# A decoder layer with attention, a state-space scan and a feed-forward net: scan, gate and feed-forward in halves of 256 tokens

## The chip, the core and the metric

The program runs on one core of a Trainium2 chip. Its engines work side by side and meet at semaphores: TensorE (PE in the profile; PEld is its weight load) multiplies matrices into PSUM, VectorE (DVE) does elementwise work, reductions and scans, ScalarE (ACT) activations, GpSimd (POOL) here only tiny powers and the DMAs that add, SyncE (SP) issues loads and stores. The metric is the device time of one execution in microseconds (us). Three runs of the kernel before took 1647.77, 1651.23 and 1653.64 us, median 1651.23.

## The reference

Four batches of 512 tokens with 512 features, all float32. First attention (16 query heads, 2 key heads, rotary positions, causal softmax) is added to x. Then a state-space block reads a context, is gated by the normed x, and is added. Last comes a feed-forward net with two of eight low-rank experts a token. The core of the scan, for each of 512 channels and 16 states n:

```python
def step(state, inp):
    d, b, c, u = inp
    dA = jnp.exp(d[..., None] * A)
    state = state * dA + (d * u)[..., None] * b[:, None, :]
    y = jnp.einsum('bdn,bn->bd', state, c)
    return (state, y)
_, ys = jax.lax.scan(step, state0, (dt_t, B_t, C_t, u_t))
```

The output y (channels by tokens) is multiplied by silu of the normed x, read as 512 rows by 512 columns: a row of the normed x is a channel of y, a column a token. The feed-forward net computes silu(x Wg) * (x Wu) over 1408 inner features, with adapters for both chosen experts, and a down product, also with adapters.

## The kernel before

Tokens stand in four tiles of 128 (NT), channels in four tiles of 128 (JT), the 1408 inner features in eleven tiles of 128 (FT). Each engine has its own program, written out by hand in the order in which it shall run. The order of the scan's work among the rest is set by tables (`plan`, PLAN_FIRST, PLAN_NEXT): each slot of the program gets some **pieces**.

The scan of a batch has 60 pieces on VectorE. Twelve of them, `poly`, evaluate the logarithm in softplus over all 2048 elements a partition and end in dt and dt*u. Then, for each of the 16 states n, follow `mul` (dt*u times B, L1086), `run` (the scan along the tokens, all four channel tiles in one row of 2048, L1091) and `out` (times C, L1096). ScalarE makes the decay factors for each n (L583) and loads the rows of B and C. GpSimd adds each product to y by an accumulating DMA of 1 MB (L487), each waiting for the one before; `mul` of n waits for the add of n - 2, whose buffer it takes.

A batch goes through these stages:

- **attention**: 32 steps (two heads at a time, key width growing from 128 to 512), each with scores (L820, L823), maximum (L1126), exponentials (L625), transposes and value products; then four output projections (L873), the first sum and the norm of x for the gate.
- **start** of the feed-forward: the gated y (L1179, L1183) is turned (L882), added (L1191), normed (L1028), turned again (L765); the router's logits (L924) go to VectorE, which picks two experts by some twenty tiny operations (L1215 to L1241); masks are turned (L934) and multiply the low-rank product (L940).
- **tiles**: for each inner tile f the base passes (L894: gate and up, four products each, 16 passes in the trace, since a float32 product is two passes), the adapters of the first and second expert (L906), the adapters' down part (L914). After each of the three, ScalarE and VectorE evaluate gate times up (L677, L1260, L1267). 33 such evaluations a batch. `base` of f + 2 waits for the last evaluation of f, whose PSUM banks it takes.
- **down**: eleven products (L974), with the next batch's query, key and value projections between them, then the sums that end the batch (L1280), on which the next attention's first scores wait.

The next batch's context part (input projection, convolution, dt) and most of its scan are done beside the feed-forward of the batch before: 30 pieces in the tiles, 22 in the down stage, 8 in attention. Batch 0 has no feed-forward before it: 13 pieces stand beside its projections, 47 in its attention. The last batch's feed-forward has no scan beside it.

## Time and profile before

| | us |
|---|---|
| median of three runs | 1651.23 |
| the profiled execution | 1649.75 |
| its span, first to last instruction | 1647.9 |
| TensorE busy | 1406.0 |
| VectorE busy | 1218.4 |
| ScalarE busy | 604.9 |
| adding DMAs (1 MB), issue to landing, median | 9.7 |

The mean granted TensorE clock was 0.876 of full speed. The span runs from the first to the last instruction of one profiled execution; the run's own time is 1.85 longer. Of a group of instructions the rows give busy time, mean duration, and how long its engine stood idle before them and what ended that.

### The profile page before, as it was taken

Reading aid. Unit: us, or ns where it says so; the run is one execution under the profiler, and the core shown is the slowest. Engines: PE = TensorE matmul, PEld = TensorE weight load, DVE = VectorE, ACT = ScalarE, POOL = GpSimd, SP = SyncE. Lnnn points to the kernel's source line nnn. Section 1 sums busy time; section 2 is a strip of 40 time slices with the busy share of each in tenths; the row PEclk is TensorE's granted clock in tenths of the full one; section 3 lists DMA queues with packets and bytes.
Section 4 is the critical chain, followed back from the end, with each engine's and each line's share of the span. In section 5 each row is a group of like instructions: output and inputs, shape, how many; then the busy total and the mean of one; then the engine's idle time right before and its main releaser. Section 6 shows DMA issues by size and latency. Waiting matters only on the chain.

```text
span 1647.9 us, 16148 instructions
## 1 busy us (share of the span) xinstructions
PE 1406.0 (85%) x5768; PEld 685.0 (42%) x5768; DVE 1218.4 (74%) x1411; ACT 604.9 (37%) x1436; POOL 111.9 (7%) x116
## 2 busy tenths in 40 slices
PE   5756767999888799899889699899879788799999
PEld 2333433443333354444334255444334345454434
DVE  4899996589989766759998865759998967623330
ACT  5165553323223584232232376242333267211110
POOL 0000001001100000000110000100210000100000
PEclk8855558999999699899999779899999869789999
DMA  4167761123666631112656822012556741101112
GB/s 185 39 147 153 154 141 27 44 66 108 143 141 166 166 66 26 39 50 78 159 128 159 196 68 52 26 37 84 124 131 152 173 135 27 26 13 64 48 32 83
DMA packets 53278, 158.81 MB, mean 96 GB/s; under 512 B 5072, under 2 KB 10704, under 8 KB 44752
## 3 DMA queue, kind: packets, MB, share of 16 engines
q0 software_dynamic: 9216, 67.11, 19.8%
q1 hardware_dynamic: 25664, 54.23, 9.9%
q10 hardware_dynamic: 18320, 36.45, 8.6%
q8 instruction: 47, 0.77, 0.2%
q14 instruction: 31, 0.25, 0.0%
HBM read 86.20 MB, written 4.46 MB: 55 GB/s over the span
## 4 chain that ended last, share of the span: by engine, by line
DVE 30%; issue 30%; PE 29%; DMA 6%; ACT 4%; POOL 2%; DVEq 0%; ACTq 0%; POOLq 0%
DVE state L1091 11%; DMA y_sb<-state 5%; PE ps_a L894 5%; DVE state L1086 4%; PE ps_a L974 4%; PE ps_a L820 3%; DVE state L1096 3%; PE ps_b L834 3%; PE ps_w L873 3%; PE ps_a L906 3%; POOL rstd L477 2%; PE ps_b L914 2%; PE ps_w L782 2%; ACT r L625 2%; DVE neg_max L1126 2%
## 5 line engine op out<-in xcount | busy, mean ns | idle before, releaser
L894 PE MATMUL ps_a<-xt,w_sb 128*128 128x512 f32 x704 | 319.2, 607 | 0.0
L1091 DVE TENSOR_TENSOR_SCAN state<-decay,state 128x2048 f32<-128x2048 f32 x64 | 282.8, 4418 | 5.3 <-ACT decay L583 0.5
L677 ACT ACTIVATE r<-ps_a 128x512 f32<-128x512 f32 x132 | 78.6, 596 | 380.6 <-PE ps_a L906 202.8
L894 PEld LDWEIGHTS ps_a<-xt,w_sb 128*128 128x128 f32 x704 | 138.1, 197 | 174.9 <-issue 174.9
L820 PE MATMUL ps_a<-r 32*128 32x512 f32 (+3 forms) x512 | 140.4, 634 | 81.7 <-ACT r L625 55.2
L906 PE MATMUL ps_a<-r,wb_sb 128*128 128x512 f32 x352 | 177.1, 628 | 35.9 <-DVE r L1267 33.7
L583 ACT ACTIVATE decay<-dt_sb,decay_rate 128x511 f32<-128x511 f32 x256 | 162.9, 712 | 104.9 <-DVE state L1096 72.2
L1260 DVE SCALAR_TENSOR_TENSOR r<-r,ps_a 128x512 f32<-128x512 f32 x132 | 89.9, 681 | 146.3 <-ACT r L677 146.3
L625 ACT ACTIVATE r<-ps_a,neg_max 128x128 f32<-128x128 f32 (+3 forms) x256 | 133.6, 534 | 116.6 <-DVE neg_max L1126 116.1
L974 PE MATMUL ps_a<-wd_sb,r 128*128 128x512 f32 x352 | 162.4, 613 | 0.0
L1086 DVE TENSOR_TENSOR state<-du_sb,bc_sb 128x2048 f32<-128x2048 f32 x64 | 146.3, 2286 | 4.7 <-DMA y_sb<-state 4.6
L1096 DVE TENSOR_TENSOR state<-state,bc_sb 128x2048 f32<-128x2048 f32 x64 | 145.9, 2280 | 0.7
L834 PE MATMUL ps_b<-cst,r 128*128 128x128 f32 x640 | 121.4, 333 | 26.0 <-ACT xt L637 16.8
L906 PEld LDWEIGHTS ps_a<-r,wb_sb 128*128 128x128 f32 x352 | 67.4, 197 | 131.1 <-issue 124.7
L1126 DVE TENSOR_REDUCE neg_max<-ps_a 128x2 f32<-128x256 f32 (+3 forms) x128 | 104.0, 814 | 21.1 <-PE ps_a L823 20.2
L487 POOL DMA_DIRECT2D y_sb<-state x64 | 56.1, 876 | 752.5 <-DVE state L1096 676.9
L974 PEld LDWEIGHTS ps_a<-wd_sb,r 128*128 128x128 f32 x352 | 70.1, 200 | 88.8 <-issue 86.8
L834 PEld LDWEIGHTS ps_b<-cst,r 128*128 128x128 f32 x640 | 89.9, 174 | 34.7 <-issue 29.5
L914 PE MATMUL ps_b<-r,ad_sb 128*128 128x512 f32 x176 | 89.8, 635 | 13.5 <-DVE r L1267 13.5
L820 PEld LDWEIGHTS ps_a<-r 32*128 32x128 f32 x512 | 49.9, 237 | 118.4 <-ACT r L625 77.2
L1267 DVE TENSOR_TENSOR r<-r,ps_a 128x512 f32<-128x512 f32 x132 | 90.7, 687 | 9.6
L477 POOL TENSOR_TENSOR rstd<-var_eps,cst 128x1 f32<-128x1 f32 x48 | 56.0, 1167 | 576.4 <-DVE var_eps L1024 576.4
(120 smaller groups left out, 1475.7 us busy)
## 6 DMA issues: line engine op xcount, KB each, us to landing
y_sb<-state POOLq DMA_DIRECT2D x64, 1024.0 KB, 9.7
bc_sb<-bc_rows ACTq DMA_DIRECT2D x64, 512.0 KB, 5.1
w_sb<-in_w_tiles SPq DMA_DIRECT2D x44, 512.0 KB, 3.7
wd_sb<-in_w_down SPq DMA_DIRECT2D x44, 256.0 KB, 3.5
wb_sb<-in_w_adapt SPq DMA_DIRECT2D x44, 128.0 KB, 2.1
xa<-in_x SPq DMA_DIRECT2D x4, 1024.0 KB, 5.2
out_x<-xb SPq DMA_DIRECT2D x16, 256.0 KB, 7.0
xn_att<-in_ctx_t SPq DMA_DIRECT2D x4, 512.0 KB, 6.1
```

The lines of the kernel that those rows point to most:

```text
L583: nc.scalar.activation(decay[:, n % 2, j, 1:L], dt_sb[:, j, 1:L], ACT.Exp, scale=decay_rate[:, j, n:n + 1]).then_inc(decay_ready, 1)
L625: nc.scalar.activation(probs[:, (2 * s + k) % 4, 0:(i + 1) * P], score_place(s, k), ACT.Exp, bias=neg_max[:, s % 2, k:k + 1], accum_out=ro ...
L820: nc.tensor.matmul(score_place(s, k), q_t[rows, m, i * P:(i + 1) * P], k_t[rows, 0:width], start=True, stop=False, tile_position=(rows.sta ...
L834: mm = nc.tensor.transpose(ps_b[:, k, kt * P:(kt + 1) * P], probs[:, (2 * s + k) % 4, kt * P:(kt + 1) * P], ident)
L894: mm = nc.tensor.matmul(ps_a[:, 2 * (f % 2) + half, :], w_sb[:, slot, at + k * P:at + (k + 1) * P], xt[:, k, :], start=(k == 0), stop=Fals ...
L906: mm = nc.tensor.matmul(ps_a[:, 2 * (f % 2) + half, :], wb_sb[:, f % 2, at:at + P], low[:, 2 * half + k - 1, :], start=False, stop=(k == 2 ...
L914: mm = nc.tensor.matmul(ps_b[:, k - 1, :], ad_sb[:, f, :], hk[:, (2 * f + k - 1) % 4, :], start=(f == 0), stop=(f == FT - 1), skip_group_c ...
L974: mm = nc.tensor.matmul(ps_a[:, i, :], hb[:, f, i * P:(i + 1) * P], wd_sb[:, f % 2, :], start=(f == 0), stop=False, skip_group_check=True)
L1086: tt(state[:, n % 2, :, :], du_sb[:], row, ALU.mult).then_inc(scan_chain, 1)
L1091: nc.vector.tensor_tensor_scan(flat, decay[:, n % 2, :, :].rearrange("p j l -> p (j l)"), flat, 0.0, ALU.mult, ALU.add).then_inc(scan_chai ...
L1096: tt(state[:, n % 2, :, :], state[:, n % 2, :, :], row, ALU.mult).then_inc(scan_chain, 1)
L1126: nc.vector.tensor_reduce(neg_max[:, s % 2, :], both, AX.X, ALU.max, negate=True)\
```

## The change

Everything behind attention is done in **units** of 256 tokens, two a batch (`HALVES = 2`, `HL = 256`).

- *Scan.* `mul`, `run` and `out` work on 4 x 256 tokens. For the first half, the last state of each channel goes to a small table `carry`; for the second half it is copied into column 0 of the state, where the first half has a zero. Each unit has 48 such pieces; the twelve `poly` pieces stay at full width, once a batch. `out` writes to a buffer of its own (`prod`), which the adding DMA reads, so now `out` of n waits for the add of n - 2. An add carries 512 KB, a load of B and C 256 KB.
- *Where the pieces stand.* First half: 12 `poly` in the evaluations 6 to 17 of the second unit before, 20 in its down stage, 28 in the steps of attention (batch 0: 13 and 47, as before). Second half: 14 in eleven slots z0 to z10 between the end of attention and the first unit's masks, 26 in the evaluations of the batch's own first unit, 8 in its first five down slots.
- *Gate.* One operation gates a half for all rows (`gate_y`), after that half's last add. The second unit's gate stands ahead of the sums that close the first (`finish`).
- *Feed-forward.* Two inner tiles share one step (`pair_tiles`): gate and up of a tile stand side by side in one PSUM bank, so one evaluation covers 2 x 256 columns. There are 18 evaluations a unit, the last pair has one tile. Base, adapter and low-rank products stream 256 columns. Weight tiles are loaded once a unit, so twice a batch, into four buffers instead of two.
- *Next batch.* Its context part stands beside the second unit alone: `project_x` at evaluation 2, dt at 4 and 5, the four attention norms at 9, 11, 13 and 15.

```diff
+HALVES = 2
+HL = L // HALVES
+HT = NT // HALVES
+UNITS = BATCH * HALVES
+FP = (FT + 1) // 2
+WS = 4
...
+STATE_PIECES = [(kind, n) for n in range(NS) for kind in ("mul", "run", "out")]
+Z_COUNTS = [1, 1, 1, 1, 1, 1, 2, 1, 2, 1, 2]
...
+            _where = list(zip([("e", _u - 1, e) for e in range(6, EVALS)], spread_over(NPOLY + 2, EVALS - 6)))
+            _where += list(zip([("d", _u - 1, f) for f in range(FT)], spread_over(20, FT)))
+        _rest = len(_pieces) - sum(count for _, count in _where)
+        _where += list(zip([("s", _b, s) for s in range(STEPS - 1)], spread_over(_rest, STEPS - 1)))
+    else:
+        _where = list(zip([("z", _b, k) for k in range(ZSLOTS)], Z_COUNTS))
+        _where += list(zip([("e", _u - 1, e) for e in range(1, EVALS)], spread_over(26, EVALS - 1)))
+        _rest = len(_pieces) - sum(count for _, count in _where)
+        _where += list(zip([("d", _u - 1, f) for f in range(5)], spread_over(_rest, 5)))
...
+            def base(u, p):
+                if p >= 2:
+                    pe.wait_ge(h_ready, u * EVALS + EVAL_AT[p - 2, 2] + 1)
+                elif u > 0:
+                    pe.wait_ge(x3_ready, HT * u)
+                for w, f in enumerate(pair_tiles(p)):
+                    q = u * FT + f
+                    pe.wait_ge(w_loaded[q % WS], 16 * (q // WS + 1))
+                    for half, at in ((0, WG), (1, WU)):
+                        for k in range(KT):
+                            mm = nc.tensor.matmul(ps_a[:, pair_bank(p) + w, half * HL:(half + 1) * HL],
+                                                  w_sb[:, q % WS, at + k * P:at + (k + 1) * P], xt2[:, k, :],
+                                                  start=(half == 0 and k == 0), stop=False, skip_group_check=True)
...
+                if kind == "mul":
...
+                    if h > 0:
+                        dve.wait_ge(carried, b * NS + n + 1)
+                        nc.vector.tensor_copy(state[:, slot, :, 0:1], carry[:, n, :].unsqueeze(2)).then_inc(edge_ready, 1)
...
+            def gate_y(u):
+                b, h = divmod(u, HALVES)
+                cols = slice(h * HL, (h + 1) * HL)
+                dve.wait_ge(z_chain, b * NT + NT)
+                dve.wait_ge(y_added, 16 * NS * (u + 1))
+                stt(silu_z[:, :, cols], y_sb[:, h, :, :], 0.5, silu_z[:, :, cols], ALU.mult, ALU.mult)\
+                    .then_inc(gated_ready, 1)
...
+                    weigh_down(u)
+                    for f in range(FT):
+                        if c is not None:
+                            rotate(c, f)
+                        pieces(("d", u, f))
+                    if first:
+                        gate_y(u + 1)
+                    finish(u)
```

On TensorE, this is the start of a feed-forward before, from the last output projections to the second base product (L739 is the next batch's input projection, L747 and L756 its x and dt products):

```order
L873 MATMUL ps_w<-wo_sb,r 128x512 x8
L739 MATMUL ps_w<-xn_att,win_sb 128x512 x6
L882 MATMUL ps_w<-cst,r 128x128 x16
L739 MATMUL ps_w<-xn_att,win_sb 128x512 x2
L765 MATMUL ps_w<-cst,r 128x128 x16
L924 MATMUL ps_b<-wr_sb,xt 128x8 x16
L894 MATMUL ps_a<-xt,w_sb 128x512 x8
L934 MATMUL ps_w<-cst,r 128x128 x16
L940 MATMUL ps_w<-xt,lora_sb 128x512 x8
L747 MATMUL ps_b<-state,wx_sb 128x512 x4
L906 MATMUL ps_a<-r,wb_sb 128x512 x2
```

And this is the same place after, for the first unit of a batch (L904 output projection, L915 and L923 the two turnings, L930 router, L944 base, L976 masks, L984 low-rank, L956 adapters):

```order
L904 MATMUL ps_w<-wo_sb,r 128x512 x8
L915 MATMUL ps_w<-cst,silu_z 128x128 x8
L923 MATMUL ps_w<-cst,r 128x128 x8
L930 MATMUL ps_b<-wr_sb,r 128x8 x8
L944 MATMUL ps_a<-r,w_sb 128x256 x16
L976 MATMUL ps_w<-cst,r 128x128 x8
L984 MATMUL ps_w<-r,lora_sb 128x256 x8
L956 MATMUL ps_a<-r,wb_sb 128x256 x4
```

The next batch's products have moved to the second unit; what is left has half the columns, and the whole sequence comes twice a batch.

On VectorE, in the tiles before, one full period of an inner tile, once the scan pieces have begun (L1260 and L1267 are an evaluation):

```order
L1260 SCALAR_TENSOR_TENSOR r<-r,ps_a 128x512
L1267 TENSOR_TENSOR r<-r,ps_a 128x512
L1086 TENSOR_TENSOR state<-du_sb,bc_sb 128x2048
L1091 SCALAR_TENSOR_TENSOR state<-decay,state 128x2048
L1260 SCALAR_TENSOR_TENSOR r<-r,ps_a 128x512
```

And in the first unit's tiles after (L1300 and L1305 an evaluation, L1143 `out`, L1122 the carry's copy, L1125 `mul`, L1132 `run`):

```order
L1300 SCALAR_TENSOR_TENSOR r<-r,ps_a 128x512
L1305 TENSOR_TENSOR r<-r,ps_a 128x512
L1143 TENSOR_TENSOR area<-area,bc_sb 128x1024
L1300 SCALAR_TENSOR_TENSOR r<-r,ps_a 128x512
L1305 TENSOR_TENSOR r<-r,ps_a 128x512
L1122 COPY area<-carry 128x4
L1125 TENSOR_TENSOR area<-du_sb,bc_sb 128x4x256
L1132 SCALAR_TENSOR_TENSOR area<-area 128x1028
```

The whole pieces between two evaluations have become half pieces, in turn one and two behind each evaluation.

Between the end of attention and the router, VectorE now has pieces too. Before, from the last gated tile:

```order
L1179 SCALAR_TENSOR_TENSOR r<-r 128x512
L1183 SCALAR_TENSOR_TENSOR r<-y_sb,r 128x512
L1191 TENSOR_TENSOR xb<-ps_w,xa 128x512
L1018 BN_STATS stats<-xb 128x6
L1021 COPY scrap<-vec 1x1
```

After, from the last row of the gate on (L1197 silu, L1222 the gate, L1230 the second sum):

```order
L1197 SCALAR_TENSOR_TENSOR silu_z<-silu_z,r 128x512
L1143 TENSOR_TENSOR area<-area,bc_sb 128x1024
L1222 SCALAR_TENSOR_TENSOR silu_z<-y_sb,silu_z 128x4x256
L1122 COPY area<-carry 128x4
L1125 TENSOR_TENSOR area<-du_sb,bc_sb 128x4x256
L1132 SCALAR_TENSOR_TENSOR area<-area 128x1028
L1230 TENSOR_TENSOR xb<-ps_w,xa 128x512
```

Three pieces now stand between the last silu and the first second sum.

## Rows read from the trace of the kernel before

**Rows 1.** The page, engines: busy us, share of the span, instructions
```profile
PE 1406.0 (85%) x5768; PEld 685.0 (42%) x5768; DVE 1218.4 (74%) x1411; ACT 604.9 (37%) x1436; POOL 111.9 (7%) x116
```
**Rows 2.** Busy time by stage: attention 0, a round's four stages, last start, tiles
```profile
core 0: us, PE busy (x) PEld busy (x) DVE busy (x) ACT busy (x) POOL busy (x), PEclk, DMA share, GB/s
...
81.00:266.00 185.00, 124.08 (x824) 70.14 (x825) 172.84 (x140) 100.04 (x273) 15.52 (x18) 0.59 0.64 139
...
1038.00:1086.00 48.00, 40.88 (x139) 21.32 (x138) 36.31 (x86) 13.96 (x26) 3.67 (x5) 0.89 0.10 33
1086.00:1238.00 152.00, 137.34 (x317) 59.65 (x316) 126.97 (x115) 49.12 (x83) 15.33 (x10) 0.97 0.38 99
1238.00:1323.00 85.00, 69.69 (x161) 30.75 (x159) 77.94 (x44) 23.36 (x37) 6.07 (x7) 0.90 0.72 163
1323.00:1424.00 101.00, 93.91 (x832) 53.83 (x832) 64.25 (x109) 64.22 (x214) 4.71 (x6) 0.83 0.29 72
1424.00:1471.00 47.00, 33.25 (x113) 21.29 (x113) 24.53 (x70) 6.54 (x12) 3.67 (x5) 0.70 0.04 12
1471.00:1603.00 132.00, 128.81 (x292) 56.23 (x293) 43.97 (x64) 19.10 (x32) 0.00 (x0) 0.98 0.15 45
```
**Rows 3.** Instructions in time, PE, tiles of the third round: start, us, engine, operation
```profile
1125.70 7.03 PE L894 MATMUL ps_a<-xt,w_sb 128*128 128x512 f32 x16
...
1137.72 7.03 PE L894 MATMUL ps_a<-xt,w_sb 128*128 128x512 f32 x16
...
1192.39 7.03 PE L894 MATMUL ps_a<-xt,w_sb 128*128 128x512 f32 x16
...
1205.70 1.96 PE L906 MATMUL ps_a<-r,wb_sb 128*128 128x512 f32 x4 [2.84 <-DVE r L1267]
1207.49 7.03 PE L894 MATMUL ps_a<-xt,w_sb 128*128 128x512 f32 x16
```
**Rows 4.** Groups of instructions: busy us, mean ns, idle before
```profile
L1091 DVE TENSOR_TENSOR_SCAN state<-decay,state 128x2048 f32<-128x2048 f32 x64 | 282.8, 4418 | 5.3 <-ACT decay L583 0.5 <-DVE state L1086 0.5
...
L1086 DVE TENSOR_TENSOR state<-du_sb,bc_sb 128x2048 f32<-128x2048 f32 x64 | 146.3, 2286 | 4.7 <-DMA y_sb<-state 4.6
...
L1267 DVE TENSOR_TENSOR r<-r,ps_a 128x512 f32<-128x512 f32 x132 | 90.7, 687 | 9.6
```
**Rows 5.** Instructions in time, DVE, a scan piece in the tiles
```profile
1167.21 2.29 DVE L1086 TENSOR_TENSOR state<-du_sb,bc_sb 128x2048 f32<-128x2048 f32 x1
1169.63 4.42 DVE L1091 TENSOR_TENSOR_SCAN state<-decay,state 128x2048 f32<-128x2048 f32 x1
1173.97 0.66 DVE L1260 SCALAR_TENSOR_TENSOR r<-r,ps_a 128x512 f32<-128x512 f32 x1
```
**Rows 6.** Instructions in time, DVE, first and last operations of the router
```profile
1061.94 0.19 DVE L1215 TENSOR_REDUCE rs<-ps_b 128x4 f32<-128x32 f32 x1 [3.91 <-PE ps_b L924]
...
1066.45 1.43 DVE L1241 TENSOR_SCALAR r<-rt 128x512 f32<-128x512 f32 x4
```
**Rows 7.** Instructions in time, PE, start of the third round's feed-forward
```profile
1061.68 10.03 PE L894 MATMUL ps_a<-xt,w_sb 128*128 128x512 f32 x16
1071.55 1.04 PE L934 MATMUL ps_w<-cst,r 128*128 128x128 f32 x8
...
1085.48 1.95 PE L906 MATMUL ps_a<-r,wb_sb 128*128 128x512 f32 x4 [0.73 <-issue]
```
**Rows 8.** Instructions in time, POOL, three adds in attention 0
```profile
165.71 0.89 POOL L487 DMA_DIRECT2D y_sb<-state  x1 [10.48 <-DVE state L1096]
176.51 0.88 POOL L487 DMA_DIRECT2D y_sb<-state  x1 [9.91 <-DMA y_sb<-state]
186.72 0.87 POOL L487 DMA_DIRECT2D y_sb<-state  x1 [9.33 <-DVE state L1096]
```
**Rows 9.** Instructions of tile y_sb, the adds' time to landing
```profile
DMA to landing us min/median/max: 6.9/9.7/12.1
```
**Rows 10.** DMA queues from 81 to 256: packets, MB, share of 16 engines
```profile
q0 software_dynamic: 2272, 16.65, 46.0%
```
**Rows 11.** Instructions in time, PE, first scores of batch 3
```profile
1322.94 0.80 PE L820 MATMUL ps_a<-r 32*128 32x128 f32 x4 [8.29 <-DVE xb L1280]
```

1212 lines of the change are left out of this document (643 added, 569 removed).

## Prediction

> **What bounds the kernel now.** I read the page's engine line first [rows 1]: TensorE is busy 85% of the span, VectorE 74%, so neither alone bounds it. The table by stage [rows 2] tells where each does. Numbers are microseconds. The span falls into: opening, 0 to 81; attention of batch 0, 81 to 266; then three equal rounds, of which the third is in the table; and the last feed-forward, 1424 to 1648. A round has four stages: the **start** (gated y turned, second norm, router, masks: 1038 to 1086), the **tiles** (1086 to 1238), the **down product** with the next batch's projections (1238 to 1323) and the **attention** (1323 to 1424). That is 48, 152, 85 and 101, in all 386. In attention 0 VectorE is busy 172.8 of 185, with most of a batch's scan in it: VectorE bounds that stage. In the tiles it is busy 127 of 152, in the down product 78 of 85. The last feed-forward is TensorE's: 128.8 of 132 in its tiles, VectorE 44.
>
> The pace of the tiles tells who leads. While VectorE has polynomial pieces only, the 16 base passes begin every 12.02 us; once whole scan pieces stand between the gate steps, every 15.10 [rows 3], and the adapter product waits 2.84 for VectorE.
>
> **Prices.** One state index n is a product, the scan and a second product on VectorE, 2286, 4418 and about 2286 ns [rows 4]. In sequence the first takes 2.42 until the scan starts, the scan 4.34 until the next operation [rows 5], the second some 2.2: 8.96. An operation over 512 elements takes 687 ns and over 2048 2286 ns [rows 4], which is 0.155 fixed and 1.04 ns an element, and 2.08 for the scan. The halves are therefore 1.22, 2.29 and 1.22; in sequence, with one copy of the carry (0.16, as any tiny operation), 1.35 + 0.1 + 2.25 + 1.15 = **4.85** for half an n. A batch's 16 n cost 155 instead of 143: +12, in four batches +48 of VectorE work. The router's tiny operations run eight times instead of four: 4.5 from its first to its first wide one and 1.35 for the four wide ones [rows 6]; only the wide ones shrink. Two tiles sharing a gate step keep the step at 512 elements: nothing gained or lost there.
>
> A matmul pass over 512 columns takes 0.43 (16 in 7.03, the last one's latency included) and one over 128 (eight in 1.04) about 0.11 [rows 3, 7]. On that line 256 columns take 0.214. There are twice as many passes at half the length: TensorE's own work stays. This width does not occur in full rows, so its bounds are 0.214 and 0.214 plus an exposed load; I take the former since the 128-column row leaves no room for a load beside it.
>
> **Attention 0.** 47 of the 60 pieces stand in it before and after, whole before, half after. Saved: 15.7 n by 8.96 − 4.85 = 64 of VectorE. The last 24 of the stage (four output projections after the last score) are TensorE's and stay. Attention of batch 3 shows what VectorE has of its own: 64 busy less 24 for its eight pieces and some 9 in those last 24, so 31 in the scoring part [rows 2]. With 76 of half pieces that is 107. The stage becomes 131: **−54**. Bounds: 121 (all 64 gained) and 148 (the adds pace it, below).
>
> **The adds.** Each piece `out` is added to y by a chained DMA: 10.2 and 10.8 apart in attention 0 [rows 8], 9.7 from issue to landing, 6.9 at best [rows 9], and 5.0 of pure transfer (46.0% of 175 us over 16 adds) [rows 10]. Halved: between 3.5 (all halves) and 9.7 (nothing does). I take 5.7, the transfer halved off the middle of 6.9 and 9.7. At 5.7 the chain is behind VectorE only when three n follow each other closely, at the end of a first-half unit. The Trainium skill, DMA: Bandwidth & Descriptors, section "Anatomy of one DMA", gives a fixed part of about 2.0 us; an estimate by it would be 2.0 and half of 7.7, 5.9, which would move the sum by under 2.
>
> **A round after.** It has two units. I followed who waits for whom with the prices above.
> - *Start of the first unit.* Now 48 from the last output projection to the first adapter product [rows 2, 7], TensorE busy 41 of it. Half the tokens make the turning, the norms and the masks half as long, but pieces z3 to z10 (11.3 of VectorE) stand in the chain: gated y at +11.8, two pieces, two sums (1.8 each), `out`, two scalings, turned by +23, router +25, router chain to +31.5, two more pieces +35, the first evaluation and the masked low product +40.5. **41**, of which TensorE works 17.
> - *Its tiles.* TensorE needs 58.4. VectorE: 17 evaluations at 1.42 (three narrow, 0.95) and 26 pieces. The pieces are not level: behind every second evaluation stand `mul` and `run` together, 3.7. From pair 2 on TensorE waits 1 to 3 each pair, and the narrow last pair, with undiminished pieces, hides nothing: **69**.
> - *The turn.* The down product of 256 tokens takes 21.5, but VectorE comes 6.5 behind, has eight pieces (13.2) and then waits for the last of three chained adds, at +28.4. Gate, the closing sums, two second sums, four convolutions (2.3 each), router, evaluation: first adapter product of the second unit at **60**, with 46 of TensorE work in it.
> - *Tiles of the second unit.* 58.4, 6.9 for the next batch's x and dt products and 1.9 of turning, 67.2. But twelve full-width polynomial pieces (2.3) and four norms (2.2) stand in its last 12 steps: VectorE 48 against TensorE's 37.8, so +11: **78**.
> - *Its down product.* 48 of TensorE; VectorE has 20 half pieces (32), five rotations (10.5) and the end, until **54**. Before, the first score waits 8.29 for VectorE's last sums [rows 11]; this shrinks to 5.
> - *Attention.* 28 half pieces (45) instead of 8 whole ones (24). With its own 31 VectorE is at 76 in the 77 of the scoring part: latencies show. **107**, bounds 101 and 116.
>
> A round: 41 + 69 + 60 + 78 + 54 + 107 = 409, which is **+23**. The tiles and the down products give back 152 + 85 − 69 − 78 − 21.5 − 54 = 14; the starts cost 41 + 38.5 − 48 = 32; attention +6. **Last batch**: 41 + 69 + 52 (turn, no convolutions) + 58.4 + 21.5 + 3 = 245 against 224: **+21**.
>
> **Sum**: 1647.9 − 54 + 3 × 23 + 21 = 1684; the profiled execution ran 1649.75 us, 1.85 over its span, so **1686** (the median of the three runs is 1651.23, 1.5 over that). Weights are loaded twice, 39 MB more; the tiles stage has its DMAs at 0.38 [rows 2] and four slots ahead, so I cost that at nothing; if this cover goes, it costs in the even down product, where a 256 KB load is due every 1.72.
>
> **Rivals.**
> - *The pieces fill waits only (faster).* In the starts VectorE waits for TensorE and ScalarE anyway. If the 9.8 of z pieces that I put on the path and the 10 by which my first-unit tiles exceed 58.4 were both hidden, four batches would give back 79: 1607. It decides at half of that: below 10 a batch left of these 20, the kernel is faster. For it: VectorE has 22.5 free in the 47 of the last start [rows 2]. Against: these waits lie before the router, the pieces after. With part hidden I set it at 1618.
> - *Adds and the clock (slower still).* Granted clock is 0.70 in the last start and 0.89 in the third round's [rows 2]; there the 16 base passes take 10.03, not 7.03 [rows 3, 7]. Eight starts with more idling: 3 each, 24, and adds landing at 7.1 rather than 5.7, 4 a batch: 16. Together 1726.
> - *Exposed weight loads.* The 1296 added passes would each show a load of about 0.11, the size of a whole 128-column pass: +143, 1829. The Trainium skill, TensorE: Matmul & The Clock Gate, section "The mechanism", says that a weight load overlaps a running matmul only where the row groups differ, which here they don't. The 0.11 of the 128-column passes speaks against it.
> - *The scheme moves nothing in sum.* Attention 0's gain is eaten exactly: 1650.
>
> **Chances.** Forecast 0.56, pieces hidden 0.26, adds and clock 0.12, exposed loads 0.02, nothing 0.04. The likeliest case's own range is 1660 to 1712. The range must hold 8 in 10 and cases of both signs: low 1628 takes in half of the faster rival, high 1728 the slower one. A measurement here tells 0.3% (5 us) from no change: faster 0.25, same 0.07, slower 0.68.
>
> **What would show each step.** Attention 0 ends near 212 and its chained adds are 6 to 8 apart. Tiles of the first unit: base passes 12 to 14 apart, 16 passes still in 3.4 to 3.6 per tile; VectorE over 90% busy. Wrong if base passes take longer than 7 us per pair (loads), if the first unit's tiles take 60 (hidden pieces), if the first adapter product follows the last output projection by under 35, or if the turn is under 50 because the last add lands early. If a round is shorter than 397, the kernel is faster.

## The result: 4.5% slower, and twice the loss that was forecast

| | us |
|---|---|
| before, median (of 4 runs beside the changed kernel) | 1652.43 |
| changed, median of 4 runs | 1726.62 (1722.59 to 1731.23) |
| ratio | 1.0455, 95% interval 1.0418 to 1.0492 |
| the profiled execution, and its span | 1722.59, 1720.8 |
| forecast, range | 1686, 1628 to 1728 |

The sign was right and the range held the time. The loss was forecast as 35 and is 74; what has to be explained is 37 us of span, 1684 against 1720.8.

The page of the changed kernel. TensorE is busy 19 longer than in [rows 1], VectorE 38; both shares are lower, so the time went into waiting.

```profile
PE 1424.9 (83%) x7064; PEld 951.9 (55%) x7064; DVE 1256.1 (73%) x1843; ACT 654.4 (38%) x1708; POOL 175.0 (10%) x180
...
L944 PE MATMUL ps_a<-r,w_sb 128*128 128x256 f32 x1408 | 337.6, 400 | 30.9 <-DVE r L1305 30.7
...
L1132 DVE TENSOR_TENSOR_SCAN area<-area 128x1028 f32<-128x1028 f32 x128 | 293.7, 2294 | 9.8 <-DVE area L1125 0.5
...
y_sb<-area POOLq DMA_DIRECT2D x128, 512.0 KB, 5.5
w_sb<-in_w_tiles SPq DMA_DIRECT2D x88, 512.0 KB, 5.0
bc_sb<-bc_rows ACTq DMA_DIRECT2D x128, 256.0 KB, 3.6
```

The prices held: the scan takes 2294 ns for a half (forecast 2.29, against 4418 in [rows 4]), the adds land in 5.5 (forecast 5.7, against 9.7 in [rows 9]). The base passes are L944.

The table by stage answers to [rows 2]. Its lines are: attention 0; then batch 1 with the start of its first unit, that unit's tiles, its down product, the second unit's start (with the down product this is the turn), the second unit's tiles, its down product; the next attention; the last batch's second start.

```profile
core 0: us, PE busy (x) PEld busy (x) DVE busy (x) ACT busy (x) POOL busy (x), PEclk, DMA share, GB/s
82.50:204.10 121.60, 103.55 (x832) 58.03 (x832) 112.27 (x166) 89.54 (x283) 17.37 (x19) 0.78 0.55 130
622.80:663.40 40.60, 21.42 (x90) 18.17 (x89) 34.56 (x67) 10.19 (x23) 6.35 (x7) 0.66 0.39 91
663.40:738.10 74.70, 63.76 (x273) 53.68 (x274) 55.92 (x64) 22.31 (x48) 6.61 (x8) 0.95 0.66 180
738.10:760.60 22.50, 21.92 (x54) 9.97 (x53) 18.27 (x18) 3.80 (x9) 2.96 (x4) 1.00 0.85 204
760.60:800.60 40.00, 27.64 (x105) 19.50 (x103) 22.33 (x55) 10.24 (x18) 2.44 (x3) 0.79 0.22 66
800.60:882.40 81.80, 72.43 (x304) 58.20 (x305) 53.83 (x70) 21.41 (x38) 10.10 (x4) 0.96 0.30 102
882.40:937.70 55.30, 47.22 (x118) 21.10 (x116) 45.41 (x49) 17.80 (x39) 5.23 (x6) 0.95 0.50 116
937.70:1047.00 109.30, 99.02 (x832) 56.08 (x832) 83.95 (x140) 77.63 (x252) 11.85 (x13) 0.81 0.38 84
1602.70:1636.50 33.80, 21.07 (x88) 17.85 (x89) 13.77 (x43) 2.98 (x6) 2.20 (x3) 0.70 0.19 51
```

Set against the terms of the sum, over all batches (measured between the first and last TensorE rows of each stage):

| term | forecast | measured | miss |
|---|---|---|---|
| opening | 81 | 82.5 | +1.5 |
| attention 0 | 131 | 121.6 | -9.4 |
| 4 starts of a first unit | 164 | 161.7 | -2.3 |
| 4 tiles of a first unit | 276 | 295.5 | **+19.5** |
| 3 turns and the last one | 232 | 242.3 | **+10.3** |
| 3 tiles of a second unit | 234 | 246.6 | **+12.6** |
| 3 down products | 162 | 165.8 | +3.8 |
| 3 attentions | 321 | 320.6 | -0.4 |
| last tiles, down product, end | 83 | 84.3 | +1.3 |

The sum of the misses is 36.9. So three terms have to be explained, 42 us, less what attention 0 gave back. One of the signs that the prediction named for its first units' tiles failed at once: VectorE was to be over 90% busy there and was busy 55.92 of 74.70, 75%.

**What the rows say about them.** In the first unit's tiles of batch 1 the two engines wait in turn. VectorE's waits there (engine, tile, line, releaser: us, times, longest):

```profile
DVE r L1300 <- ACT r L718: 14.8, 5, 4.4
DVE area L1125 <- DMA bc_sb<-bc_rows: 1.7, 1, 1.7
```

L1300 begins an evaluation; L718 is its tanh, and behind that stand TensorE's base passes. TensorE's own waits for VectorE are 12 in the same stage. One of them, in time, with the base passes behind it:

```profile
679.71 8.85 PE L944 MATMUL ps_a<-r,w_sb 128*128 128x256 f32 x32 [3.31 <-DVE r L1305]
```

The same 32 passes take 7.07 elsewhere. 3.31 is a wait for the evaluation (0,2), in front of which VectorE runs a scan; 8.85 is the price of the granted clock, which was 0.62 from 679 to 682 after it. The base passes came at 679.71, 693.57, 708.17 and 720.36, 12.2 to 14.6 apart: the forecast had 12 to 14.

In the start of the first unit TensorE works at 0.50 of its clock (1.2 GHz) after two long waits: eight transposes 1.97 instead of 1.04 [rows 7], the base passes 9.58. Instructions in time, TensorE, start of batch 1 (start, us, engine, line, operation, count, wait before):

```profile
633.44 1.97 PE L915 MATMUL ps_w<-cst,silu_z 128*128 128x128 f32 x8 [10.61 <-DVE silu_z L1222]
642.23 1.97 PE L923 MATMUL ps_w<-cst,r 128*128 128x128 f32 x8 [6.82 <-DVE r L1072]
644.04 3.58 PE L930 MATMUL ps_b<-wr_sb,r 128*128 128x8 f32 x16
647.47 9.58 PE L944 MATMUL ps_a<-r,w_sb 128*128 128x256 f32 x32
```

In the turn the two projections of the next batch (L785) pay it, 6.40 instead of 3.60:

```profile
774.81 1.97 PE L923 MATMUL ps_w<-cst,r 128*128 128x128 f32 x8 [6.50 <-DVE r L1072]
776.61 3.58 PE L930 MATMUL ps_b<-wr_sb,r 128*128 128x8 f32 x16
780.04 6.40 PE L785 MATMUL ps_w<-xn_att,win_sb 128*128 128x512 f32 x8
```

and VectorE waits for the last of the chained adds before the gate, 8.3 to 9.0 in each of the four:

```profile
755.78 1.23 DVE L1143 TENSOR_TENSOR area<-area,bc_sb 128x1024 f32<-128x1024 f32 x1
765.93 1.23 DVE L1222 SCALAR_TENSOR_TENSOR silu_z<-y_sb,silu_z 128x1024 f32<-128x1024 f32 x1 [8.92 <-DMA y_sb<-area]
```

### The profile page after: what moved, and what is told of

It reads as the page before. It is cut to its first block, busy times and chain, and to the rows that moved or that the text cites. A ratio compares the mean times of both kernels' runs of the same rounds, so it can differ in the third digit from the quotient of the medians.

```text
span 1720.8 us, 20050 instructions
## 1 busy us (share of the span) xinstructions
PE 1424.9 (83%) x7064; PEld 951.9 (55%) x7064; DVE 1256.1 (73%) x1843; ACT 654.4 (38%) x1708; POOL 175.0 (10%) x180
## 3 DMA queue, kind: packets, MB, share of 16 engines
q1 hardware_dynamic: 44672, 94.60, 16.6%
## 4 chain that ended last, share of the span: by engine, by line
PE 48%; DVE 29%; DMA 7%; ACT 7%; issue 6%; POOL 1%; ACTq 0%; DVEq 0%; PEld 0%; SPq 0%; POOLq 0%; PEldq 0%
PE ps_a L944 17%; DVE area L1132 7%; DMA y_sb<-area 5%; PE ps_a L956 4%; PE ps_w L821 4%; PE ps_a L1027 3%; DVE area L1143 3%; PE ps_a L854 3%; PE ps_b L868 3%; DVE area L1125 3%; DVE neg_max L1171 2%; ACT area L613 2%; PE ps_b L965 2%; DVE du_sb L1097 2%; PE ps_w L904 2%
## 5 line engine op out<-in xcount | busy, mean ns | idle before, releaser
L944 PE MATMUL ps_a<-r,w_sb 128*128 128x256 f32 x1408 | 337.6, 400 | 30.9 <-DVE r L1305 30.7
L944 PEld LDWEIGHTS ps_a<-r,w_sb 128*128 128x128 f32 x1408 | 282.2, 202 | 83.4 <-DVE r L1305 39.5
L1132 DVE TENSOR_TENSOR_SCAN area<-area 128x1028 f32<-128x1028 f32 x128 | 293.7, 2294 | 9.8 <-DVE area L1125 0.5
L613 ACT ACTIVATE area<-dt_sb,decay_rate 128x256 f32<-128x256 f32 x512 | 217.3, 502 | 123.3 <-DVE area L1143 74.6
L1300 DVE SCALAR_TENSOR_TENSOR r<-r,ps_a 128x512 f32<-128x512 f32 x144 | 91.6, 636 | 206.7 <-ACT r L718 206.5
L718 ACT ACTIVATE r<-ps_a 128x512 f32<-128x512 f32 x144 | 80.4, 560 | 396.9 <-PE ps_a L956 206.0
L520 POOL DMA_DIRECT2D y_sb<-area x128 | 112.0, 875 | 1011.4 <-DVE area L1143 755.2
L956 PE MATMUL ps_a<-r,wb_sb 128*128 128x256 f32 x704 | 175.0, 392 | 30.4 <-DVE r L1305 15.5
L956 PEld LDWEIGHTS ps_a<-r,wb_sb 128*128 128x128 f32 x704 | 135.2, 195 | 59.8 <-DVE r L1305 20.8
L1125 DVE TENSOR_TENSOR area<-du_sb,bc_sb 128x1024 f32<-128x1024 f32 x128 | 155.7, 1217 | 9.5 <-DMA bc_sb<-bc_rows 9.2
L1143 DVE TENSOR_TENSOR area<-area,bc_sb 128x1024 f32<-128x1024 f32 x128 | 156.2, 1220 | 1.0 <-DMA y_sb<-area 0.6
L1171 DVE TENSOR_REDUCE neg_max<-ps_a 128x2 f32<-128x256 f32 (+3 forms) x128 | 104.3, 815 | 12.2 <-PE ps_a L857 11.8
L1027 PEld LDWEIGHTS ps_a<-wd_sb,r 128*128 128x128 f32 x352 | 66.5, 192 | 81.6 <-issue 72.1
L868 PEld LDWEIGHTS ps_b<-cst,r 128*128 128x128 f32 x640 | 88.6, 172 | 34.1 <-issue 31.1
L965 PE MATMUL ps_b<-r,ad_sb 128*128 128x256 f32 x352 | 88.0, 392 | 23.4 <-DVE r L1305 23.4
L1305 DVE TENSOR_TENSOR r<-r,ps_a 128x512 f32<-128x512 f32 x144 | 92.5, 643 | 9.8 <-DVE r L1300 0.5
```

What stands on the lines that cost most here:

```text
L613: nc.scalar.activation(decay[:, g % 2, j, 1:SW], dt_sb[:, j, h * HL:(h + 1) * HL], ACT.Exp, scale=decay_rate[:, j, n:n + 1]).then_inc(deca ...
L868: mm = nc.tensor.transpose(ps_b[:, k, kt * P:(kt + 1) * P], probs[:, (2 * s + k) % 4, kt * P:(kt + 1) * P], ident)
L944: mm = nc.tensor.matmul(ps_a[:, pair_bank(p) + w, half * HL:(half + 1) * HL], w_sb[:, q % WS, at + k * P:at + (k + 1) * P], xt2[:, k, :], ...
L956: mm = nc.tensor.matmul(ps_a[:, pair_bank(p) + w, half * HL:(half + 1) * HL], wb_sb[:, q % WS, at:at + P], low[:, half, k - 1, :], start=F ...
L965: mm = nc.tensor.matmul(ps_b[:, 0, (k - 1) * HL:k * HL], ad_sb[:, f, :], hk[:, (2 * p + k - 1) % 4, w, :], start=(f == 0 and k == 1), stop ...
L1027: mm = nc.tensor.matmul(ps_a[:, OUT_BANK[i], :], hb[:, f, i * P:(i + 1) * P], wd_sb[:, q % WS, :], start=(f == 0), stop=False, skip_group_ ...
```

## The experiments

Four theories came out of this. **A**: TensorE's low clock after its waits. **B**: who waits for whom in the tiles, set by where the pieces stand. **C**: the weights, loaded twice, crowd the adds and the loads of B and C rows. **D**: the last add in each turn. Each experiment ran beside the kernel before on one chip, but they are spread over three chips; the kernel before had medians of 1651.5 to 1652.4 on them. Differences between two runs are differences of medians. Stage times below are means over the units of one profiled execution; medians are of the timed runs.

| run | median | ratio, 95% | first start | first tiles | second tiles |
|---|---|---|---|---|---|
| changed | 1726.62 | 1.0418 to 1.0492 | 40.4 | 73.9 | 82.2 |
| e3 thin second half | 1661.10 | 1.0030 to 1.0071 | 33.0 | 63.0 | 82.7 |
| e4 quarter adds | 1697.26 | 1.0257 to 1.0295 | 40.4 | 71.3 | 82.1 |
| e6 light weights | 1707.67 | 1.0302 to 1.0364 | 40.8 | 72.1 | 82.2 |
| e7 first tiles by kind | 1702.18 | 1.0271 to 1.0325 | 40.6 | 69.4 | 82.2 |
| e8 both tiles by kind | 1691.53 | 1.0186 to 1.0272 | 40.5 | 69.2 | 78.1 |
| e9 dealt again | 1689.73 | 1.0198 to 1.0272 | 40.7 | 69.3 | 76.5 |
| e10 e9 and fillings | 1652.76 | 0.9999 to 1.0051 | 37.0 | 68.2 | 76.3 |
| f1 changed and fillings | 1698.42 | 1.0239 to 1.0300 | 37.1 | 74.8 | 82.6 |
| f3 e10, last sum on VectorE | 1642.65 | 0.9911 to 0.9958 | 37.7 | 69.2 | 76.0 |

### e3: the second half's pieces cut thin

```diff
-                    tt(inner, du_sb[:, :, h * HL:(h + 1) * HL], row, ALU.mult).then_inc(scan_chain, 1)
+                    tt(inner[:, :, 0:thin], du_sb[:, :, h * HL:h * HL + thin], row, ALU.mult).then_inc(scan_chain, 1)
```
(`thin` is 16 for h = 1, else 256; `out` in the same way, and the scan of a second half covers 64 of its 1028 elements. This part of the scan is left out.)

> The changed kernel with the scan pieces of each second half cut to 16 of 256 columns (product, second product) and 64 of 1028 elements (scan), each about 0.2 instead of 1.22, 2.29 and 1.22; this part of the scan is left out, the adds and all waits stay. It shows what the pieces cost that stand in the starts of the first units, their tiles and the turn. By the prediction's terms: start 41 to 31, tiles 69 to the 58.4 of TensorE and 4 for its clock, the turn 60 to about 50 since VectorE comes to the last pieces early; 30 a batch, -120, about 1605. Theory B: more, -130 to -150, since the miss in the first units' tiles and turns goes too. Theory A: the 4 in the tiles stays, and the starts keep 0.50 of the clock: -100 to -120.

Measured: 1661.1, **-66** and not -120. The starts went from 40.4 to 33.0 and the first units' tiles from 73.9 to 63.0, as forecast for the pieces (the terms said 9.8 and 10.6; they are 7.4 and 10.9). The rival by which they fill waits only is out. But the turn did not shrink: the second units' starts went from 38.9 to 41.3, 40.0 to 39.9, 39.2 to 42.8 and 33.8 to 37.1. With nothing between them the pieces come as fast as their adds allow. From 640 to 745 the page's DMA queues were (packets, MB, share of 16 engines; q0 is the adds, q1 weights, q10 B and C)

```profile
q0 software_dynamic: 1728, 6.29, 32.5%
q1 hardware_dynamic: 4896, 10.09, 27.8%
q10 hardware_dynamic: 1441, 2.62, 7.7%
```
and the gate still waited 9.9 for the last add. So the adds stand right behind the pieces, and this much faster VectorE in the tiles gave the turn nothing.

### e4: quarter adds

(Three quarters of y are left out.)

```diff
-                    pool.dma_start(y_sb[:, h, :, :].rearrange("p j l -> p (j l)"),
-                                   prod[:, g % 2, :, :].rearrange("p j l -> p (j l)"),
-                                   accum_op=ALU.add).then_inc(y_added, 16)
+                    pool.dma_start(y_sb[:, h, 0, :], prod[:, g % 2, 0, :], accum_op=ALU.add).then_inc(y_added, 16)
```

> The changed kernel with each add moving a quarter of its product (one of four channel tiles, 128 KB); three quarters of y are left out. The add then lands in about 3 instead of 5.5. In the turn VectorE waits 8.9 for the last add; with the chain of the last adds shorter by 2.5 to 3 each, this wait falls by 5 to 8, in four turns -20 to -30; the first units' gated y by nothing. If attention 0 were paced by the adds, it would shorten too; the page's steps put it to VectorE, so it stays at 121. Together about 1700. If the adds cost nothing beyond what is hidden: 1722 to 1727.

Measured: 1697.26, **-29**. A quarter of the bytes land in 3.8 instead of 5.5 (the page, DMA issues: count, KB, median us to landing):

```profile
y_sb<-area POOLq DMA_DIRECT2D x128, 128.0 KB, 3.8
```
and the gate waits 3.2 (instructions in time, VectorE, turn of batch 1):
```profile
754.59 1.23 DVE L1220 SCALAR_TENSOR_TENSOR silu_z<-y_sb,silu_z 128x1024 f32<-128x1024 f32 x1 [3.20 <-DMA y_sb<-area]
```
The starts of the second units took 35.0, 36.6, 36.5 and 29.1 instead of 38.9, 40.0, 39.2 and 33.8: -15. First units' tiles gave 10 more, attention 0 nothing, which is VectorE's. VectorE's waits for the B and C rows fell from 9.2 to 3.4 in the whole program, so large adds also hold up other loads; the forecast had neither in the tiles. D is real: the forecast had the wait at the gate in it (the last add at +28.4; it landed at +27.8), so that wait is no part of the miss.

### e1, e2, e5, e12: filling TensorE's waits

```diff
+            def warm(name, n):
+                bank = fill(pe, name)
+                for _ in range(n):
+                    nc.tensor.matmul(ps_w[:, bank, :], ident, wo_sb[:, 0, :], start=True, stop=True)
...
+                warm(("yt", u, 0), 5 if h else 20)
                 pe.wait_ge(gated_ready, u + 1)
```

> The changed kernel with idle TensorE time filled: 512-column passes whose product nobody reads (20 in front of turning the gated y in a first unit, 5 in a second, 12 in front of turning the normed tokens, 6 and 7 at the two long waits in a first unit's tiles, 16 in front of the first score of batches 1 to 3). No result changes. Theory A (the 37 us that the forecast lacks are TensorE at 0.50 of its clock after its waits): in each start the two sets of eight transposes go from 1.97 to 1.04, the router's 16 from 3.58 to about 1.8, the base passes from 9.58 to about 7.1; 4 to 5 of these 6 us are on the path, in eight starts 36; first units' tiles 2 each, 8; the attentions' first 20 us some 3 each, 9: together -45 to -55, about 1672. Theory B (VectorE's pieces set the pace, and the low clock lies beside them): -10 or less, 1712 to 1727. If the added passes themselves delay the work, it is slower.

> The kernel before with the same filling where it idles long: 18 passes in front of the first score of batches 1 to 3, 16 in front of turning the gated y of the last batch. Its other starts have the next batch's projection in these places. Theory A: the clock costs the kernel before little, since it waits rarely: -3 in each of three attentions and -3 in the last start, about 1640. Theory B: nothing, 1652. If it comes out as much faster as the filled changed kernel, the clock is no cost of the halves and explains nothing of the miss.

Measured: 1764.62 and 1666.46, **38 slower** than the changed kernel and 15 slower than before (1.0074 to 1.0109). The dose was wrong: a product written once is two records, 0.88 in all, and the 12 before the normed tokens ran 10.6, far past the wait.

```profile
656.25 10.57 PE L783 MATMUL ps_w<-wo_sb,cst 128*128 128x512 f32 x24 [0.42 <-DVE xb L1244]
666.66 1.04 PE L932 MATMUL ps_w<-cst,r 128*128 128x128 f32 x8
```
The clock was kept (1.04 for the transposes), and the time lost anyway. These two runs say nothing for or against A.

> In the run with filled waits a 512-column pass written once shows as two records and takes 0.88, not 0.44, so the fillings were twice as long as the waits. Here they are cut to fit: 10, 3, 6, 3 and 8 passes, and 2, 3 and 3 at the last waits of a second unit's tiles. Theory A (low clock after waits is the missing 37): starts -4 each, first units' tiles -2, second units' -3, attentions -3: about -55, 1670. Theory B (who waits for whom, in the order of the pieces, sets the pace): starts -2 to -3 each, since the router's passes and the first base passes lie on the chain, tiles 0 to -1: about -20, 1705.

Measured: 1704.49 (1696.51 to 1713.25), **-22**, which is B's number and not A's; but the fillings, here at the long waits inside the tiles too, still did not fit: after ten passes TensorE was idle 2.0, then 3.0, and the six before the normed tokens began at low clock and ended 2 late; starts stayed at 40.0 to 41.2. Inconclusive on its own; f1 repeats it with a better fit.

> The kernel before with 9 passes in front of the first score of batches 1 to 3 and 8 in front of turning the last batch's gated y, half of the earlier try, which began its attentions 6 late and yet ran them in 97.8 instead of 100.5. If the low clock is worth that 2.7 and the filling now fits the waits of 9.0 and about 10: three times -2.7 and -1: about 1643, faster than both kernels. If the 2.7 came from starting late (more done beside it): 1652.

Measured: 1650.10 (1642.32 to 1659.18), ratio 0.9979 to 1.0021: **nothing**. Its attentions took 99.8, 99.3 and 106.0. The kernel before has the next batch's projections in the waits of its first three starts, which were not filled, and gains nothing from fillings in the four waits that were.

### e6, e11: light weights

```diff
+                part = WBASE // (4 if u else 1)
-                sp.dma_start(w_sb[:, q % WS, :], w_tiles[f]).then_inc(w_loaded[q % WS], 16)
+                sp.dma_start(w_sb[:, q % WS, 0:part], w_tiles[f][:, 0:part]).then_inc(w_loaded[q % WS], 16)
```
(wd_sb likewise; the feed-forward then computes with older weights. The adapters' loads stay.)

> The changed kernel with a quarter of each weight load from the second unit on (128 KB of 512 KB, 64 of 256 KB; the rest of the slot keeps older weights, so the feed-forward computes with wrong ones). In the run with thin pieces the DMA engines were busy all the time in the first units' tiles, and adds landed in 6.3. Theory C (the weights loaded twice crowd the chained adds and the loads of B and C): waits of VectorE for them, 9 in the trace, and of the gated y for the last add, 8.9 in each turn, shrink: first units' tiles -3, turns -3, attentions 0: -20 to -25, about 1700. If the cover that the prediction named holds: within 5 of 1725.

Measured: 1707.67, **-19**. The weights' queue moves 49.19 MB here, 94.60 in the changed kernel and 54.23 in the kernel before, so e6 takes away 45 where the second loading added 40. The adds' median landing did not move (5.5); VectorE's waits for the B and C rows fell from 9.2 to 4.8 in the whole program; the profiled spans differ by 15: first units' tiles -7, turns -5, the rest in the attentions, which vary anyway. The cover that the prediction named for the second loading does not hold fully, though in the changed kernel the base passes wait 0.5 for a weight and the down products 1.5, in all. (In e3 the DMA engines were 68% busy from 640 to 745, by the three queues above, and not all the time.)

> The dealt-out kernel with a quarter of each weight load from the second unit on, as in the run with light weights (the feed-forward then uses older weights). With the order mended, first units' tiles are at VectorE's 69 with the DMA engines 0.78 busy, and 3.4 of one stage are a wait for a load of B and C, 1.3 for weights. Theory C: these go, -3 to -4 in each first unit's tiles and -1.5 in each turn: -15 to -20. If crowding only mattered through the old order: -5 or less.

Measured: 1673.62 against 1689.73 of its twin e9, **-16**; first units' tiles 69.3 to 66.7, three of the four at a granted clock of 1.00. C stands with either order, at 16 to 19 by the medians; 7 and 11 of these lie in the first units' tiles.

### e7, e8, e9: the same pieces, dealt out by the kind of evaluation

```diff
+TILE_COUNTS = [3, 0, 2, 3, 0, 2, 3, 0, 2, 3, 0, 2, 3, 0, 2, 1, 0]
-        _where += list(zip([("e", _u - 1, e) for e in range(1, EVALS)], spread_over(26, EVALS - 1)))
+        _where += list(zip([("e", _u - 1, e) for e in range(1, EVALS)], TILE_COUNTS))
```

> Nothing is left out: the 26 pieces of a first unit's tiles are only dealt out by the kind of evaluation they follow. Behind the first evaluation of a pair (k = 0) none, behind k = 1 three, behind k = 2 two, instead of one or two everywhere. In the trace TensorE waits for the evaluation k = 2 of two pairs earlier, which comes right behind the pieces of the k = 0 slot, while VectorE idles 2 to 4 before each evaluation k = 0. Theory B (order): the two stop waiting for each other, first units' tiles 74 to 64 (58.4 of TensorE, the narrow last pair and one wait more), with no wait long enough for the clock to fall: four times -10, -40, about 1685. Theory A: the clock's 4 in these tiles come after the start's waits and stay; less than -15. Theory C: the adds and loads bound these tiles soon, DMA 0.66 busy goes over 0.9: -10 to -20.

Measured: 1702.18, **-24**; the four tiles stages 68.7, 69.3, 70.1 and 69.7, together 17.8 shorter, the turns 4.2. VectorE's waits in this stage of batch 1:

```profile
DVE r L1301 <- ACT r L719: 5.4, 5, 2.7
DVE area L1126 <- DMA bc_sb<-bc_rows: 2.9, 1, 2.9
```
and the stage in the table by stage:
```profile
656.60:725.80 69.20, 62.59 (x272) 52.78 (x273) 59.34 (x67) 22.04 (x48) 7.15 (x9) 0.95 0.76 204
```
14.8 of waiting for the tanh became 5.4. The stage did not go to 64. From 1086 to 1142 of this run VectorE has one operation behind the other, evaluations and pieces, beside waits of 1.3 and less and one of 3.45 for the B and C rows. In the stage of batch 1 it is busy 59.34 of 69.20 and waits 8.3, so 69 is VectorE's work, some 61 with the small gaps, and these waits. The prediction's own prices give 65 for that work (17 evaluations and 26 pieces). The granted clock is 0.95 in both, so the clock did not make this difference.

> As the run with the first units' tiles dealt out by kind, and the second units' too: the twelve-odd polynomial pieces stand behind k = 1 and k = 2 only, one and two, and the four norms of the next batch come in the steps 1, 3, 4 and 6, which hold no pieces, instead of 9, 11, 13 and 15. Nothing is left out. Theory B: second units' tiles 82 to 73 (67.2 of TensorE and some waits), three times -9, so -27 more than the other run: about 1658. Theory A: at most -5 more.

```diff
-NORM_SLOTS = (9, 11, 13, 15)
+NORM_SLOTS = (1, 3, 4, 6)
-            _where = list(zip([("e", _u - 1, e) for e in range(6, EVALS)], spread_over(NPOLY + 2, EVALS - 6)))
+            _where = list(zip([("e", _u - 1, e) for e in range(6, EVALS)], [1, 2, 0, 1, 2, 0, 1, 2, 0, 1, 2, 1]))
```
(12 `poly` and the first `mul`.) Measured: 1691.53, **-11** against e7; second units' tiles 82.2 to 78.1. Pieces and norms were moved together; which of them gave it is not separated. A new wait showed (instructions in time, ScalarE, then TensorE, end of the tiles in batch 2): the first decays (L614) wait for the last `poly`, and the copies behind them on ScalarE hold TensorE.

```profile
1275.56 1.70 ACT L614 ACTIVATE area<-dt_sb,decay_rate 128x256 f32<-128x256 f32 x4 [3.00 <-DVE area L1107]
...
1277.89 1.94 PE L810 MATMUL ps_w<-cst,xn_att 128*128 128x128 f32 x8 [4.88 <-ACT xt L624]
```

> The run with both tiles dealt out by kind, mended in one place: there ScalarE stood 3.0 at the end of a second unit's tiles with the first decays, which wait for the last polynomial piece, and TensorE 4.9 for the copies queued behind them. Here the polynomial ends one step earlier (2, 2, 0, 1, 2, 0, 1, 2, 0, 1, 2, 0 instead of 1, 2, 0, ... 1). Nothing is left out. Theory B (who waits for whom decides): second units' tiles 78 to 75, in three rounds -9: 1683. If the poly pieces' sum bounds it, as VectorE's sum bounds the first units' 69: no change, 1691.

(The loads of B and C rows may also be issued behind any evaluation here, which moves one of them a batch.) Measured: 1689.73, second units' tiles 75.7, 78.2 and 75.7, mean 76.5, **-1.6** each; by the medians 2, within their spread. B's sign, less than its size.

### e10, f1, f2: fillings that fit

```diff
+                warm(("yt", u, 0), 3 if h else 11)
...
+                warm(("xt2", u, 0), 5 if u % HALVES else 4)
...
+                        if s == 0:
+                            warm(("pv", b, 0), 8)
```

> The run before it with the starts' and attentions' waits filled by passes that nobody reads, 11 and 4 in a first unit's start, 3 and 5 in a second's, 8 before the first score; none in the tiles. The first try at this length had 2.0 and 3.0 left unfilled, and the passes before the normed tokens ended 2 too late. Theory A in its smaller form (the clock costs where TensorE's chain router, base, masks, low product lies on the path, 11.8 at full clock and 14.3 in the trace, and the 6.40 instead of 3.6 for two projections in the turn): starts -2.5, turns -3, attentions -2, in all about -25 against that run, 1658. Theory B: the start is VectorE's (34.5 busy of 40), -5 or less.

> The changed kernel as it is, with nothing but the fillings of the run that had both order and clock mended (11 and 4 passes in a first unit's start, 3 and 5 in a second's, 8 before the first score). That run was 37 faster than its twin without fillings. Theory A (the low clock after the starts' and attentions' waits is a cost of its own, whatever the order of the tiles): -30 to -37 here too, about 1692. If the fillings only pay once the tiles are dealt out by kind, since the late pieces swallow what the starts gain: -15, about 1710.

> The dealt-out kernel with the fillings of the eight starts alone, without the 8 passes before the first scores. By its trace the starts gave 3.7, 2.4, 4.2 and 4.3, the turns 2.8, 4.0, 0.8 and 0.4, together 22; the attentions of batches 1 to 3 took 102.8 in place of 111.6, 106.7 and 106.7. If the attention's part is the fillings' own (its first scores no longer at 0.50 of the clock): here attentions at 105 to 110 again and 1667. If it comes from a warm start of the round before: 1653.

Measured: e10 1652.76, **-37** against e9; f1 1698.42, **-28** against the changed kernel. A is real, at either order. Of the 44 by which the profiled spans of e9 and e10 differ, the starts give 15, the turns 8 and the three attentions 17. The start of batch 1 in e10 (L784 is the filling):

```profile
602.42 9.61 PE L784 MATMUL ps_w<-wo_sb,cst 128*128 128x512 f32 x22
613.19 1.09 PE L924 MATMUL ps_w<-cst,silu_z 128*128 128x128 f32 x8 [1.16 <-DVE silu_z L1232]
617.41 6.53 PE L784 MATMUL ps_w<-wo_sb,cst 128*128 128x512 f32 x8 [3.12 <-DVE xb L1240]
623.77 1.04 PE L933 MATMUL ps_w<-cst,r 128*128 128x128 f32 x8
625.06 1.95 PE L940 MATMUL ps_b<-wr_sb,r 128*128 128x8 f32 x16 [0.25 <-ACT r L631]
626.87 7.15 PE L954 MATMUL ps_a<-r,w_sb 128*128 128x256 f32 x32
```
Transposes 1.04 for 1.97, router 1.95 for 3.58, base 7.15 for 9.58; of these 5 us 3.4 are on the path (starts 40.4 to 37.0; 37.1 in f1). In f1 the turns took 60.5, 59.2, 57.2 and 56.4, together 9.0 less than in the changed kernel; the first units' tiles took 0.9 more each, so the low clock of the starts is no part of *their* miss. f1 fills no wait inside the tiles; e5 did, and its first units' tiles took 72.5 for 73.9.

f2, without the passes before the first scores, ran 1661.96 (1.0033 to 1.0094), 9 slower than e10, though the two intervals overlap. Its profiled attentions took 103.1, 102.8 and 111.5. Attentions of the same code took 102.4 to 111.6 in these runs, with fillings ahead of them and without; in e10 all three took 102.7 to 102.8. Whether the passes do this, or the state in which the stage is entered, stays open; it is up to 9 us.

### f3: the last sum on VectorE

```diff
+                    if h == 1 and g % NS == NS - 1:
+                        pool.dma_start(scrap_d[:], prod[0:1, g % 2, 0, 0:1]).then_inc(y_added, 16)
+                        continue
...
+                    dve.wait_ge(y_added, 16 * NS * (u + 1) - 16)
+                    dve.wait_ge(scan_chain, 3 * NS * (u + 1))
+                    tt(y_sb[:, h, :, :], y_sb[:, h, :, :], prod[:, (NS - 1) % 2, :, :], ALU.add).then_inc(y_whole, 1)
...
+                    mask_low(u)
                     if c is not None:
                         convolve(c, 3)
-                    mask_low(u)
```
(Nothing is left out. The filling of three passes before the gated y of a second unit goes too.)

> The dealt-out and filled kernel, and two more edits, nothing left out: the last of a batch's 16 adds of the second half is no DMA but a VectorE sum in front of the gate (1.2 of VectorE; the queue moves one element instead), and in the start of a second unit the masked low product comes before the fourth convolution, not behind it; no filling before the gated y of a second unit. In the trace of the changed kernel VectorE waits 8.3 to 9.0 for the last add in every turn, and TensorE 2.4 for the masked product behind the convolution. Adds theory: the gate comes 5 earlier, but TensorE is in the down product until 22 after its start and in two projections for 3.6 more, so turns get 3 to 4 shorter by it and 2.3 by the order: four times -4 and three times -2: about 1631, faster than the kernel before by 1.2%. If the start's own chain bounds the turn: 1645 to 1650.

Measured: 1642.65 (ratio 0.9911 to 0.9958 against before), **-10** against e10: 0.6% faster than the kernel before, though not by the 22 expected. The wait at the gate is 3.2 instead of 8.3, and with the sum of 1.23 in front of it the gate follows the last product at 5.7 instead of 9.5:

```profile
723.73 1.23 DVE L1158 TENSOR_TENSOR area<-area,bc_sb 128x1024 f32<-128x1024 f32 x1
728.14 1.23 DVE L1241 TENSOR_TENSOR y_sb<-y_sb,area 128x1024 f32<-128x1024 f32 x1 [3.19 <-DMA y_sb<-area]
729.40 1.23 DVE L1243 SCALAR_TENSOR_TENSOR silu_z<-y_sb,silu_z 128x1024 f32<-128x1024 f32 x1
```
The second starts took 30.5, 30.6, 34.0 and 28.0 for 35.9, 34.2, 37.4 and 31.1, -15.5 in sum; the first units' tiles took 4 more, the first starts 2, and one attention 106.3 for 102.7. What the sum and what the earlier masked product gave is not separated.

## Why the forecast was right in sign and wrong in size

**The tiles of a first unit, 69 a unit: the step that failed.** "From pair 2 on TensorE waits 1 to 3 each pair" looked at TensorE's waits only, and took VectorE to be busy throughout. VectorE's work is 65 by the prediction's prices, and e7 reaches 69 with these pieces in a better order, with 8.3 of waits left. In the order of the change VectorE stands 14.8 a stage before its evaluations, because a scan stands behind the evaluation k = 0, right in front of the k = 2 that frees TensorE's next base passes; while these run, VectorE has nothing. The two idle in turn. Dealing the same pieces by kind gives back 17.8 of the 19.5. The kernel before had its table in just this form (`IN_EVALS` takes `(0, 2, 1)[k]` for the kinds k = 0, 1, 2), and the change puts an even spread in its place (`spread_over(26, EVALS - 1)`), which I did not price. Part of the stage is also the price of the weights (below): e11 runs it in 66.7.

**The tiles of a second unit, 78.** The same step: "VectorE 48 against TensorE's 37.8, so +11" adds up one engine's load, and the evenly spread `poly` and norms stand before the evaluations that TensorE waits for. With the pieces and norms moved 82.2 became 76.5; that covers the whole miss (4.2 each).

**The turn, 60 and 52.** The chain up to the gate was right: the last add at +27.8 (forecast +28.4). The 31.6 behind it was priced at full clock and took 34.6, with 2.8 of it in the projections at 0.50. The three turns with projections missed by 6.1, and the fillings of f1 take 9.2 from them. The last turn missed by 4.3, and f1 leaves it as it was, with 5.1 still unfilled before its first transposes and a filling behind them that ends late. Its rows put the clock there too:

```profile
1615.67 2.10 PE L923 MATMUL ps_w<-cst,r 128*128 128x128 f32 x8 [3.42 <-DVE r L1072]
1617.57 3.49 PE L930 MATMUL ps_b<-wr_sb,r 128*128 128x8 f32 x16
1620.91 9.27 PE L944 MATMUL ps_a<-r,w_sb 128*128 128x256 f32 x32
```
That is 4.7 more than 1.04, 1.95 and 7.15, but no run shows it as the cause of this turn's miss. I had put the clock into a rival only.

**The start, 41.** Measured 40.4, right by luck, from two errors: the pieces in it cost 7.4 and not 9.8 (e3), and the low clock, which was not in the sum, costs 3.4 (e10, f1). The "11.3 of VectorE" for z3 to z10 was a wrong sum as well: these are eleven pieces, 18 at the prediction's own prices and 17.7 in the trace of batch 1.

**Weights loaded twice, cost at nothing.** Without most of them the kernel is 16 to 19 faster (e6, e11). 7 and 11 of this lie in the first units' tiles, where adds, weights and B and C loads meet (DMA 0.66 of the stage, against 0.38 in [rows 2]), 5 and 3 in the turns, which hold the even down product where I looked, and the rest is within what the attentions vary. It acts inside the miss of the tiles: the terms of A, B and C overlap and their sum, some 80, is not the miss.

**The down products, 54.** 55.3 each. The wait of the first scores, forecast as 5, was 7.87:

```profile
937.67 0.80 PE L854 MATMUL ps_a<-r 32*128 32x128 f32 x4 [7.87 <-DVE xb L1319]
```
That is more than the 1.3 missed; what made up for the rest is open.

**Attention 0, 131.** Measured 121.6. VectorE is busy 99.0 of the 102.0 of the scoring part, as forecast, which had 107 there; and the part from the first output projection behind the last score took 19.6 and not 24, which the trace of before could have told (19.0, 19.3 and 19.6 in its attentions of batches 1 to 3; 26.0 in attention 0). By the marks used here attention 0 of the kernel before ends at 269.8 and not at the 266 of the prediction, so it took 188.4 and the halves save 67.

**Adds, 256-column passes, pieces.** 5.5 for 5.7, 7.07 for 32 passes (0.22 each), 2.29 and 1.22: right. Exposed weight loads are out: 32 passes with 32 loads over the full array take 7.07, the time of 16 passes of double width [rows 3]. The Trainium skill, TensorE: Matmul & The Clock Gate, section "The mechanism", has a line by which a load overlaps a running matmul only in other row groups; the trace does not agree with it for these float32 passes. The same section also lets a load for the background weight buffer go ahead of running matmuls, which would fit, though no run here tells that apart.

**The rivals.** "Adds and the clock" gave 1726, the time measured, but for reasons that hold by half: the clock costs 28 (24 there), while the adds landed in 5.5 and not in the 7.1 to which its 16 belonged. What adds do cost beyond the forecast is in the first units' tiles, 10 at most (e4). That the time agrees does not make it the cause. "Pieces fill waits" is out by e3: 18 of its 20 a batch are on the path.

## What to carry to other kernels

Where two engines hand work to each other in a loop, price the order and not the load: write down, for each piece placed between two steps, which step of the *other* engine becomes late by it, and what the first engine does meanwhile. Splitting work in halves doubles every start; a start costs its chain and then the low clock of the engine that waited, and passes that nobody reads can buy that back only if they end before the wait does: too long by 5 us they cost more than the clock. When a prediction's time agrees with the measurement, check the terms: here two right numbers stood on wrong parts.
